# A two-layer graph network with two mixtures of experts on one core: rows gathered and added in token order in place of sorted copies

## The reference

```python
x = x + gnn0(layernorm(x), edges)    # per node one edge: softmax over 4 heads, mix of 64 channels
x = x + ffn0(layernorm(x))           # router, top 2 of 6 experts, three 256x256 layers, relu
x = x + gnn1(layernorm(x), edges)    # graph attention over all edges, segment softmax, relu
x = x + ffn1(layernorm(x))           # gate, top 2 of 8 experts, 256 -> 1024 -> 256, gelu
```

## Time and profile before

| | us |
|---|---|
| median of 3 runs | 2877.5 |
| lowest, highest | 2876.17, 2878.03 |
| the profiled execution | 2876.24 |
| its span | 2874.6 |
| PE busy (x13130) | 2056.5 |
| DVE busy (x4111) | 1554.9 |
| POOL busy (x1463) | 1426.2 |
| ACT busy (x2579) | 936.1 |
| bytes moved by DMA | 293.06 MB |

### The profile page before, as it was taken

The page is one execution under the profiler, slowest core; times in us unless marked ns, Lnnn a source line. Parts: engine busy times, 40 slices in busy tenths (PEclk is TensorE's granted clock), DMA queues, the critical chain, the costliest instruction groups (busy, mean ns, idle before and its releaser), DMA issues. The chain is left out here.

```text
span 2874.6 us, 54757 instructions
## 1 busy us (share of the span) xinstructions
PE 2056.5 (72%) x13130; PEld 1850.7 (64%) x13131; DVE 1554.9 (54%) x4111; ACT 936.1 (33%) x2579; POOL 1426.2 (50%) x1463
## 2 busy tenths in 40 slices
PE   2623328998475888877888788786519999999990
PEld 2423217898354666666666666665519999999990
DVE  5366525665473655555555555556624545555445
ACT  1333315676241111111111111112315555555540
POOL 1257753434104777777777777773761223232230
PEclk9855558999686888888888888886559999999995
DMA  6312243333353444444444444443251222121117
GB/s 157 102 45 78 76 116 92 105 102 98 105 169 93 112 112 114 112 114 114 112 114 113 110 115 112 112 114 87 103 141 46 72 73 73 55 91 51 62 37 268
DMA packets 234820, 293.06 MB, mean 102 GB/s; under 512 B 101917, under 2 KB 185524, under 8 KB 234540
## 3 DMA queue, kind: packets, MB, share of 16 engines
q0 software_dynamic: 72016, 202.56, 24.3%
q1 hardware_dynamic: 149222, 76.37, 10.5%
q10 hardware_dynamic: 13544, 13.73, 1.4%
HBM read 214.72 MB, written 78.22 MB: 102 GB/s over the span
## 5 line engine op out<-in xcount | busy, mean ns | idle before, releaser
L1553 POOL DMA_INDIRECT at_G<-h_as,at_idx x850 | 807.1, 950 | 269.2 <-issue 266.7
L1704 PE MATMUL at_pAgg<-at_G,at_OH 128*128 128x260 f32 x1700 | 542.6, 485 | 159.8 <-DVE at_ACC L1602 95.5
L1704 PEld LDWEIGHTS at_pAgg<-at_G,at_OH 128*128 128x128 f32 x1700 | 404.8, 246 | 261.5 <-DVE at_G L1584 179.0
L1169 POOL DMA_INDIRECT expert_out<-e_ob,e_to x212 | 221.6, 1045 | 560.6 <-DVE e_ob L1380 392.4
L1304 ACT ACTIVATE e_full<-e_pH,g_bias_hidden 128x256 f32<-128x256 f32 x640 | 316.0, 494 | 357.4 <-PE e_pH L1202 344.6
L1662 ACT ACTIVATE at_OT<-at_pTr 128x384 f32<-128x384 f32 (+1 forms) x300 | 125.7, 470 | 657.2 <-PE at_pTr L1689 656.9
L1364 DVE TENSOR_TENSOR e_hT_low<-e_full,e_hT_high 128x256 fp32r<-128x256 f32 x536 | 263.2, 503 | 130.6 <-ACT e_hT_high L1305 130.5
L1584 DVE TENSOR_TENSOR at_G<-at_G,at_pIds 128x1536 f32<-128x1536 f32 x150 | 249.7, 1665 | 153.5 <-ACT at_pIds L1669 153.5
L1200 PE MATMUL e_pH<-e_xT_high,e_WA_high 128*128 128x256 f32 x1072 | 309.1, 288 | 3.9 <-DVE e_WA_low L1359 3.0
L1201 PE MATMUL e_pH<-e_xT_low,e_WA_high 128*128 128x256 f32 x1072 | 306.8, 286 | 0.0
L1202 PE MATMUL e_pH<-e_xT_high,e_WA_low 128*128 128x256 f32 x1072 | 305.0, 285 | 0.0
(11 more groups left out here) (301 smaller groups left out, 3635.7 us busy)
## 6 DMA issues: line engine op xcount, KB each, us to landing
e_xs<-slot_rows SPq DMA_DIRECT2D x109, 257.0 KB
at_G<-h_as,at_idx POOLq DMA_INDIRECT x850, 2.8
b_rows<-expert_out SPq DMA_DIRECT2D x14, 896.0 KB
f_rows<-expert_out ACTq DMA_DIRECT2D x14, 896.0 KB, 6.9
g_raw_first<-in_L_ffn_W_dram POOLq DMA_DIRECT2D x8, 1024.0 KB, 5.3
g_raw_last<-in_L_ffn_W_dram POOLq DMA_DIRECT2D x8, 1024.0 KB
xt_ar<-a_og SPq DMA_DIRECT2D x7, 910.0 KB, 4.5
h_as<-b_og SPq DMA_DIRECT2D x7, 910.0 KB, 4.2
```

The costliest lines, as they stand in the source:

```text
L1169: gp.indirect_dma_start(K.YS, bass.IndirectOffsetOnAxis(ap=to[b][:, s:s + 1], axis=0), ob[b][:, s, :], None).then_inc(sent[b], 16)
L1553: gp.indirect_dma_start(G[j][:, c, :], None, K.T1, bass.IndirectOffsetOnAxis(ap=idx[j][:, c:c + 1], axis=0)).then_inc(gathered[j], 16)
L1704: last = nc.tensor.matmul(pAgg[:, 0:DIM + 4], OH[j][:, c, :], G[j][:, c, :], start=(j == 0 and c == 0), stop=(j == NJ - 1 and c == CHUNKS[ ...
```

## The change

The normed rows are stored in token order (`K.YN`, 260 floats: the row, the two experts, the two weights), and so is the residual, in `K.XD`, with a second sum `K.XE`, which is zeroed in a1. The slots are turned around into tables `K.SRC` and `K.TO` (source and target row of each slot) without a scatter: DVE makes one-hot rows of a slot's low 7 bits, POOL those of its upper bits times the node's code, and PE multiplies them (`trace`: 14 products of 128 x 312 columns a trip in a1, 416 in b1), accumulating in one bank; DVE decodes it (`sources`). In `experts` POOL copies two columns of `K.SRC` and gathers two times 128 rows, four to six tiles ahead; DVE picks the weight of each slot (`shares`), ACT scales the product by it (`scale`), DVE adds the weighted bias, and POOL scatters with an addition in DRAM: in e0 each half of a tile to a sum of its own, in e1 both to `K.XD`, the second after the first has landed. `update` in b0 loads both sums into two buffers and adds them in one operation of 1792 columns; `finish` is a copy of `K.XD` to the output by two DMAs. The rows in a1 are free after the products with them, not after the additions to x. At a change of expert POOL splits the last weights first.

```diff
 def project(K, tag, pre, x=None, gat_weights=None, router=None, gate=None):
+                    with sp.Fori(0, TRIPS) as i:
...
+                        sp.wait_ge(meta_ready, i + 1)
+                        sp.sem_inc(passed, 1)
+                        sp.dma_start(K.YN[bass.ds(r0, BODY * P), :].rearrange("(t p) c -> p t c", p=P),
+                                     kept[:, bass.ds(part, BODY), :]).then_inc(stored, 16)
+                        sp.dma_start(K.XD[bass.ds(r0, BODY * P), :].rearrange("(t p) c -> p t c", p=P),
+                                     K.X[:, bass.ds(i * BODY, BODY), :]).then_inc(stored, 16)
+                        if router:
+                            sp.dma_start(K.XE[bass.ds(r0, BODY * P), :].rearrange("(t p) c -> p t c", p=P),
+                                         zeros[:, :].rearrange("p (o d) -> p o d", o=1).to_broadcast([P, BODY, DIM])).then_inc(stored, 16)
-                def scatter(i, k):
+                def highs(i):
                     gp.wait_ge(slots_ready, i + 1)
-                    freed(gp, y_kept, (i + 1) * BODY)
-                    if k == 1:
-                        gp.wait_ge(moved, i + 1)
-                    for t in range(i * BODY, (i + 1) * BODY):
-                        gp.indirect_dma_start(K.XS, bass.IndirectOffsetOnAxis(ap=K.POS[:, t, k:k + 1], axis=0),
-                                              Y[:, t, :], None).then_inc(sent[k], 16)
+                    freed(gp, traced, i)
+                    for j in range(BODY):
+                        t = i * BODY + j
+                        for k in range(2):
+                            n = 2 * j + k
+                            nc.gpsimd.tensor_scalar(high[:, n, :], K.iota[:, 0:E * COLS], at_high[:, n:n + 1], K.code[:, t:t + 1],
+                                                    ALU.is_equal, ALU.mult).then_inc(highs_ready, 1)
-                        for j in range(BODY):
-                            ch.mark(nc.vector.scalar_tensor_tensor(Xt, rows[:, 0, j, :], Wt[:, 0:1], Xt, ALU.mult, ALU.add))
-                        ch.settle()
-                        for j in range(BODY):
-                            nc.vector.scalar_tensor_tensor(Xt, rows[:, 1, j, :], Wt[:, 1:2], Xt,
-                                                           ALU.mult, ALU.add).then_inc(rows_used, 1)
+                        V.tensor_tensor(Xt, Xt, second[:, b:b + BODY, :], ALU.add).then_inc(rows_used, 1)
+                    if not isinstance(i, int) or i > 0:
+                        weights(i - 1)
+                    V.tensor_tensor(gap[:, :, :], top[:, :, 1:2], top[:, :, 0:1], ALU.subtract).then_inc(gap_in, 1)
...
+                    ch.link(V.tensor_copy(posi[:, :], place_at))
+                    ch.link(V.tensor_scalar(highi[:, :], posi[:, :], 7, None, ALU.arith_shift_right))
+                    freed(v, highs_ready, i * (2 * BODY))
+                    ch.link(V.tensor_copy(at_high[:, :], highi[:, :]))
+                    ch.link(V.scalar_tensor_tensor(at_low[:, :], at_high[:, :], -float(P), place_at, ALU.mult, ALU.add))
+                    v.sem_inc(slots_ready, 1)
+                    freed(v, traced, i)
+                    V.tensor_tensor(low[:, :, :], K.iota[:, 0:P].rearrange("p (o n) -> p o n", o=1).to_broadcast([P, 2 * BODY, P]),
+                                    at_low[:, :].rearrange("p (n o) -> p n o", o=1).to_broadcast([P, 2 * BODY, P]),
+                                    ALU.is_equal).then_inc(lows_ready, 1)
+                def trace(i, last):
+                    pe.wait_ge(lows_ready, i + 1)
+                    for n in range(2 * BODY):
+                        freed(pe, highs_ready, i * (2 * BODY) + n + 1)
+                        ins = nc.tensor.matmul(pI[:, 0:E * COLS], low[:, n, :], high[:, n, :],
+                                               start=False, stop=(last and n == 2 * BODY - 1))
+                    ins.then_inc(traced, 1)
                 def trip(i):
                     for j in range(BODY + 2):
+                        if routed and j == 1 and not isinstance(i, int):
+                            trace(i - 2, False)
 def experts(K, tag, E, H, func, deep):
+        sums = (K.XD, K.XE) if deep else (K.XD, K.XD)
+                def gather(t, b):
+                    at = field(gp, t, 1, E * COLS - SUB)
+                    if not isinstance(t, int) or t >= 2:
+                        freed(gp, pX_ready, t - 1)
+                        freed(gp, share_ready, t - 1)
+                    gp.sem_inc(passed, 1)
+                    nc.gpsimd.tensor_copy(source[b][:, :], K.SRC[:, bass.ds(at, SUB)]).then_inc(source_ready, 1)
+                    gp.wait_ge(source_ready, t + 1)
+                    gp.sem_inc(passed, 1)
+                    for s in range(SUB):
+                        gp.indirect_dma_start(xs[b][:, s, :], None, K.YN,
+                                              bass.IndirectOffsetOnAxis(ap=source[b][:, s:s + 1], axis=0)).then_inc(x_in[b], 16)
+                def scatter(t, b):
+                    for s in range(SUB):
+                        freed(gp, o_ready, t * SUB + (s + 1))
+                        if not deep and s > 0:
+                            gp.wait_ge(sent[s - 1], t * 16 + 16)
+                        gp.sem_inc(passed, 1)
+                        gp.indirect_dma_start(sums[s], bass.IndirectOffsetOnAxis(ap=to[b][:, s:s + 1], axis=0),
+                                              ob[b][:, s, :], None, compute_op=ALU.add).then_inc(sent[s], 16)
+                def trip(i, b, more):
+                    t = i * 2 + b
+                    if more:
+                        gather(t + (D + 4), (b + D) % 2)
+                    freed(gp, tile_done, t + 1)
...
+                        split_last(e)
+                        next_last(e)
...
+                        landed(t)
+                        gp.sem_inc(ob_free, 1)
+                    scatter(t, b)
+                def scale(t):
+                    at = slice(t, t + 1) if isinstance(t, int) else bass.ds(t, 1)
+                    freed(act, o_ready, t * SUB)
+                    freed(act, share_ready, t + 1)
+                    freed(act, tile_done, t + 1)
+                    for s in range(SUB):
+                        nc.scalar.activation(scaled[:, s, :], pO[s][:, 0:DIM], ACT.Copy,
+                                             scale=share[:, at, s:s + 1].rearrange("p o s -> p (o s)")).then_inc(scaled_ready, 1)
-                        V.tensor_tensor(ob[b][:, s, :], pO[s][:, 0:DIM], W.bias["l"][:, bass.ds(e, 1), :].rearrange("p o d -> p (o d)"),
-                                        ALU.add).then_inc(o_ready, 1)
+                        freed(v, scaled_ready, t * SUB + (s + 1))
+                        V.scalar_tensor_tensor(ob[b][:, s, :], W.bias["l"][:, bass.ds(e, 1), :].rearrange("p o d -> p (o d)"),
+                                               share[:, bass.ds(t, 1), s:s + 1].rearrange("p o s -> p (o s)"), scaled[:, s, :],
+                                               ALU.mult, ALU.add).then_inc(o_ready, 1)
 def finish(K, out):
+        part = (TILES - 1) // 2 * P
+        def move(eng, a, rows, signal):
+            eng.dma_start(out[a:a + rows * P, :].rearrange("(p r) d -> p r d", p=P),
+                          K.XD[a:a + rows * P, :].rearrange("(p r) d -> p r d", p=P)).then_inc(signal, 16)
```

More of the change, by code:

```diff
@@ L30 @@
 E1, H1 = 8, 1024
-WIDE = DIM + 1
+WIDE = DIM + 4
 NODEROWS = TILES * P
@@ L642, in _ @@
                 late = 2 if pre == "attn0" else 0
[L643 removed]
+                for i in range(TRIPS + late):
                     if pre == "attn0" and i < TRIPS:
                         gather(i)
[L646 to L652 removed]
+                    if routed and i >= late:
+                        highs(i - late)
             @block.vector
@@ L830, in _ @@
                     edges.spans(v)
-                with v.Fori(1, TRIPS - 3) as i:
-                    trip(i)
+                if pre == "reload":
+                    for i in range(1, TRIPS - 3):
+                        trip(i)
+                else:
+                    with v.Fori(1, TRIPS - 3) as i:
+                        trip(i)
                 trip(TRIPS - 3)
@@ L964, in _ @@
                     pe.wait_ge(w_in, 16 * n_w)
+                if routed:
+                    pe.wait_ge(consts, 4)
+                    nc.tensor.matmul(pI[:, 0:E * COLS].rearrange("p (c e) -> p c e", e=E), K.ones[:, :],
+                                     before[:, :].rearrange("p (o e) -> p o e", o=1).to_broadcast([P, COLS, E]), start=True, stop=False)
                 trip(0)
-                with pe.Fori(1, TRIPS) as i:
+                if routed:
+                    trip(1)
+                with pe.Fori(2 if routed else 1, TRIPS) as i:
                     trip(i)
                 if routed:
+                    trace(TRIPS - 2, False)
                     count(TRIPS - 1)
+                    trace(TRIPS - 1, True)
                 if routed:
```

(29 more changed lines are left out.)

461 lines of the change are left out of this document (235 added, 226 removed).

## The result

The changed kernel takes 3099.9 us (median of 4 runs, 3099.5 to 3100.4) where the kernel before takes 2876.8 us on the same chip: ratio 1.078 (95% interval 1.076 to 1.079). The forecast was 2836 us and faster. The profiled execution has a span of 3097.8 us, 223.2 more than before.

A forecast was written before the change was run, and what follows sets the result against it. Bounds differ by stage: POOL's DMAs in a0, attention, a1 and b1, PE in e0 and e1, DVE in b0, DMA in the finish. Terms -25 + 70 - 35 - 13 + 3 - 41 = -41 gave 2836 us, range 2785 to 2905.

The forecast's parts named there:

- I take 0.6, nearer the first, since there is one tensor operand: a1: POOL's one-hot product of 312 columns is priced at 0.6 us, within 0.36 to 0.76 us.
- b1's upper bound of 1.02 us: b1: a POOL one-hot of 416 columns costs 0.5 to 1.02 us; 22 us a trip at the upper end.
- The remark that the counting matmuls queue behind trace matmuls: a1: counting matmuls queue on PE behind 14 trace matmuls of an earlier trip, adding some 1 us a trip.
- The rule that was weighed: b1: DVE's low one-hots and POOL's products would take turns, 2 us a trip; b1 wins 3 us, not 13.
- POOL as the bound: e0: POOL needs 6.37 us a tile where PE needs 5.07, so POOL becomes the bound; e0 +70 us.
- the tile of 6.37 us: e0: POOL's tile of two scatters 2.54, two gathers 2.50, expert tests 0.66 and preparation 0.67 us.
- The preparation: e0: on POOL, the slot number, the copy of two indices and its wait, 0.67 us a tile.
- Rival A: e0: the adding scatter loads POOL twice, 1.94 us, 8.3 us a tile, +166 instead of +70, total 2932; chance 0.14.
- POOL is late once and catches up 4 us a tile: e1: at a change of expert, 7.5 us of splitting and loads delay POOL once, then it recovers; e1 +3 us.
- Rival E: e1: ScalarE's scaling is PE's wait, 0.8 us for 54 tiles, 43 us instead of 3, total 2876; chance 0.07.
- rival D: Finish: the copy from DRAM to DRAM runs at half rate, total 2853 us; chance 0.10.
- C: One-hots bind b1, POOL's at 1.02 us: b1 +10 instead of -13, a1 -5 instead of -25, total 2879; chance 0.12.

The follow-up runs named there:

- own_rows3: Changed kernel with one-hots on DVE, e0 scattering plainly to own rows, POOL gathering before landing waits, e1's second scatter behind the next gathers: 2915.5 us, ratio 1.013.

## Why the prediction was wrong

The direction was wrong, mostly by one kind of error: prices taken for operations that the trace didn't hold. The steps, by the prediction's own headings:

- **a1 and b1.** "I take 0.6, nearer the first, since there is one tensor operand" is the step that failed. The number of operands wasn't the question; the comparison was: 1.75 us for 416 columns alone. b1's upper bound of 1.02 us (22 us a trip) was too low for the same reason. With it the rest of the mechanism follows: POOL and DVE in turns over PE's queue, b1 +84.5 for -13, a1 +25.9 for -25. The remark that the counting matmuls queue behind trace matmuls was right and was priced at 1 us; it was worth whatever POOL was late. With the one-hots on DVE, a1 came to -13 and b1 to +7, though DVE then carries 5.8 us of them a trip in b1. The rule that was weighed, DVE and POOL in turns, 2 us a trip, holds in size (1.9 us), but in the trip shown it was POOL that waited, and 2 us of 32 are not what made b1 longer.
- **e0.** POOL as the bound was right, and the tile of 6.37 us stood on a plain scatter: that term failed. The adding form adds 0.68 us twice (1.65 for 0.97; left out: -69 us). The preparation, taken at 0.67 us, is worth 1.0 (moved: -52 us over 51 tiles); in it the 0.15 us for the semaphore had no row, and POOL stood 0.88. 6.37 + 1.36 + 0.35 = 8.1 us is the tile that was measured. With plain scatters and nothing else changed in e0 it takes 415 us, where the forecast, which had priced it so, says 400. The two gains overlap: own_rows3 scatters plainly and copies earlier, and wins 77 and not 121 us; that its 406 us lie near 400 is chance, since its terms are others. Rival A named this mechanism at 0.14 and set its point at a scatter of 1.39 us; it measured 1.65. Its price of 1.94 was too high, and that e0 came out near where it said (+154 against +166) is in part luck: the preparation, too low in both, made up for some of it. That POOL writes twice the descriptors, its reason, isn't shown.
- **b0.** -28.1 for -35, and inside the bounds: DVE's sum is 2.02 us as taken, but it still waits 13.3 us in all for the second array, and PE took 59.92 / 7 = 8.6 us a trip at a granted clock of 0.86, not the 7.8 of full speed.
- **e1.** +28.1 for +3, inside the bounds of -5 and +40. "POOL is late once and catches up 4 us a tile" missed that an adding scatter lands late (3.9 us after issue, where I had 2.4) and that two changes of expert come close enough behind it. Rival E was wrong: PE's last products waited 1.2 us for the scaling in all.
- **Finish.** -42.7 for -41: the copy from DRAM to DRAM takes 23.8 us, and rival D is out.

In the sum, the terms -25 and -13 for a1 and b1 were wrong by 148 us, e0 by 84, e1 by 25 and b0 by 7. The chances were wrong before the sizes: A and C hang on the same engine, each was given little because no row spoke for it, and both came true together (C by its mechanism, at nearly twice its price for a one-hot).

What stays open: why e1 takes 706 to 708 us in own_rows3 and with the one-hots on DVE, where the change has 698; how far the copy and the expert tests share their time in e0, which would say why its two gains don't add up; why the adding form costs POOL more; and what slows the attention on the other chip, and the kernel before in a1, e0 and b1 there.

## What to carry to other kernels

A price taken from rows is a bound only if a row has the same operation on the same engine. A comparison on POOL cost here 3.6 times what it cost on DVE (1.75 against 0.49 us). Before work is moved onto an idle engine, count all that it will issue a tile, waits for its own results included, and ask which in-order queue hands its delay on: here PE's queue turned POOL's 26 us a trip into DVE's wait. A change of several parts is worth taking apart: b0's two pairs of buffers alone made the kernel 13 us faster, where the whole made it 223 us slower.

## What the runs showed that I had not expected

- POOL's comparison: 1.32 us for 416 columns where multiply and add together take 0.69 us; DVE makes the whole one-hot in 0.41 to 0.49 us.
- An adding scatter takes POOL 1.58 us against 0.99, for rows of 256 and of 64 columns alike, and lands 3.9 us after its issue where a plain one lands after 2.4.
- A small copy on POOL reads 0.77 us behind an adding scatter and 0.19 behind a plain one.
- A wait of 3.1 us a tile on an engine with room to spare cost 22 us, through two changes of expert and the last tile.
